# A graph network's compare operand moves to PSUM, and the node sums move to the banks of their transposes

## The reference

```python
edge_index = stack([src, dst])
x = x + L0(relu(norm(x)), ...)   # attention: score = q[dst]*k[src] per head, softmax over the
                                 # edges of a node, sum of weight * v[src], then @ Wa
x = x + L1(relu(norm(x)), ...)   # 4 layers: relu(x[src] + silu(edge_attr @ We + be)), segment_sum
                                 # over dst, two matmuls with silu, layer norm
x = x + L2(relu(norm(x)), ...)   # 2 convolutions with degree norm: segment_sum of rows, @ W, relu
x = x + L3(relu(norm(x)), ...)   # segment_sum(x[src]) @ W + x @ W_self
```

## Time and profile before

| | |
|---|---|
| median of 3 runs | 11198.52 us (11189.39 to 11209.08) |
| profiled execution | 11231.99 us, span 11230.1 us |
| busy in the span | PE 6020.5 us (54%), DVE 3251.3 (29%), ACT 1365.6 (12%), POOL 6472.3 (58%) |
| granted PE clock, mean over the span | 0.723 of full speed |
| DMA | 960.66 MB, mean 86 GB/s |
| comparisons of L1327 | 1567.8 us busy, 1969 of them, mean 796 ns |
| gathers of L700 into `rows` | 5386.0 us busy, 5488 of them, mean 981 ns |

### The profile page before, as it was taken

One profiled execution on the slowest core, in us unless ns is written; L12 is line 12 of the kernel. 1 busy time (PEld: TensorE's weight loads), 2 busy tenths in 40 slices (PEclk: granted clock), 3 DMA queues, 4 the chain that ended last, 5 costly groups with the idle time before them and its releaser, 6 DMA issues. The chain is left out here.

```text
span 11230.1 us, 158248 instructions
## 1 busy us (share of the span) xinstructions
PE 6020.5 (54%) x23911; PEld 4066.9 (36%) x23912; DVE 3251.3 (29%) x7438; ACT 1365.6 (12%) x2091; POOL 6472.3 (58%) x6737
## 2 busy tenths in 40 slices
PE   2556646566665666756666566653344333433344
PEld 1334425433443333433344333332333233333334
DVE  2334467612232122311223122331122112221222
ACT  1112210011221112211122111210000000000000
POOL 2556526466655665556554655546666566656665
PEclk9566669877887788877888778875666555665566
DMA  4777754233322333323332322221111111111111
GB/s 112 206 208 218 219 152 129 86 85 83 84 80 73 86 82 80 82 74 86 82 80 75 83 80 79 77 57 44 46 47 47 44 44 46 44 42 44 45 46 44
DMA packets 982683, 960.66 MB, mean 86 GB/s; under 512 B 442720, under 2 KB 710395, under 8 KB 982137
## 3 DMA queue, kind: packets, MB, share of 16 engines
q0 software_dynamic: 213248, 462.82, 15.6%
q1 hardware_dynamic: 647644, 399.74, 13.3%
q10 hardware_dynamic: 121756, 97.77, 2.7%
HBM read 801.39 MB, written 164.71 MB: 86 GB/s over the span
## 5 line engine op out<-in xcount | busy, mean ns | idle before, releaser
L700 POOL DMA_INDIRECT rows<-node_rows,idx x5488 | 5386.0, 981 | 3647.5 <-SPq L550 1992.6
L1327 DVE SCALAR_TENSOR_TENSOR onehots<-iota_f,win_base,dst_ch 128x512 f32<-128x512 f32 x1969 | 1567.8, 796 | 6664.0 <-remote 3954.8
L832 PE MATMUL ps_seg<-rows,onehots 128*128 x7840 | 1584.2, 368 | 2422.8 <-DVE sums L1348 1089.9
L832 PEld LDWEIGHTS ps_seg<-rows,onehots 128*128 128x128 f32 x7840 | 1383.6, 265 | 2621.6 <-issue 2617.4
L832 PEld LDWEIGHTS ps_seg<-onehots 128*128 128x128 f32 x7840 | 1178.7, 220 | 1744.6 <-issue 962.5
L832 PE MATMUL ps_seg<-onehots 128*128 128x128 f32 x7840 | 1231.4, 307 | 1066.6 <-DVE sums L1348 466.6
L906 PE MATMUL ps_big<-q_res,ident 128*128 (+1 forms) x1968 | 1277.0, 736 | 766.1 <-issue 325.5
L906 PE MATMUL ps_big<-rows,ident 128*128 (+1 forms) x1968 | 1180.7, 686 | 2.1 <-issue 2.1
L700 POOL DMA_INDIRECT sums<-kv_rows,idx x784 | 775.2, 989 | 528.5 <-SPq L550 302.6
L1051 ACT ACTIVATE onehots<-ps_big 128x512 f32<-128x512 f32 x980 | 576.1, 597 | 3251.0 <-remote 1470.5
L906 PEld LDWEIGHTS ps_big<-rows,ident 128*128 128x128 f32 x1968 | 445.1, 227 | 616.3 <-issue 614.0
(11 more groups left out here) (193 smaller groups left out, 2243.4 us busy)
## 6 DMA issues: line engine op xcount, KB each, us to landing
q_res<-gates_by_edge SPq DMA_DIRECT2D x784, 256.0 KB
rows<-node_rows,idx POOLq DMA_INDIRECT x5488
gates_by_edge<-gate ACTq DMA_DIRECT2D x244, 256.0 KB
rows<-dst_padded SPq DMA_DIRECT2D x196, 256.0 KB
value_rows_by_edge<-sums SPq DMA_DIRECT2D x196, 256.0 KB
rows<-value_rows_by_edge SPq DMA_DIRECT2D x196, 256.0 KB, 3.1
idx<-src_padded SPq DMA_DIRECT2D x1568, 2.0 KB
node_rows<-h_res ACTq DMA_DIRECT2D x49, 448.0 KB
```

The costliest lines, as they stand in the source:

```text
L700: pool.indirect_dma_start(target[:, r, j, :], None, table, bass.IndirectOffsetOnAxis(ap=idx[:, r, j:j + 1], axis=0)).then_inc(rows_landed[ ...
L832: last = nc.tensor.matmul(ps_seg[u % 2][:, 0:width], onehots[:, u, j, :], rhs(j), start=j == 0, stop=j == J - 1)
L1327: V.scalar_tensor_tensor(onehots[:, u, :, :], iota_f[:, :].rearrange("p (a n) -> p a n", a=1).to_broadcast([P, J, P]), win_base[:, ds(w, 1 ...
```

## The change

A name `numbers` is given to the first 128 columns of bank `ps_mm[0]`. DVE copies `iota_f` into them once, just ahead of the attention pass. `mark_edges` reads its node numbers from there instead of from SBUF; its other tensor input `dst_ch`, its per-partition operand `win_base` and its output stay in SBUF. The sums of L856 are written to `ps_sum`, another name for `ps_t`, and DVE's `summed(h)` reads them there; `ps_mm[1]` is no longer used from the attention pass on.

```diff
+        numbers = ps_mm[0][:, 0:P]
+        ps_sum = ps_t
...
-                            last = nc.tensor.matmul(ps_mm[h][:, (i - a) * D:(i - a + 1) * D], left, right,
+                            last = nc.tensor.matmul(ps_sum[h][:, (i - a) * D:(i - a + 1) * D], left, right,
                                                     start=m == 0, stop=m == len(pairs) - 1)
...
+            chain(V.tensor_copy(numbers, iota_f[:, :]))
+
             def mark_edges(k, s, u, c, w):
 
                 V.scalar_tensor_tensor(onehots[:, u, :, :],
-                                       iota_f[:, :].rearrange("p (a n) -> p a n", a=1).to_broadcast([P, J, P]),
+                                       numbers.rearrange("p (a n) -> p a n", a=1).to_broadcast([P, J, P]),
                                        win_base[:, ds(w, 1)],
                                        dst_of(c).rearrange("p (j a) -> p j a", a=1).to_broadcast([P, J, P]),
                                        ALU.add, ALU.is_equal).then_inc(onehot_ready, 1)
...
-                return ps_mm[h][:, 0:(end - first) * D].rearrange("p (w d) -> p w d", d=D)
+                return ps_sum[h][:, 0:(end - first) * D].rearrange("p (w d) -> p w d", d=D)
```

## The result

The changed kernel takes 11240.85 us in the median of 19 runs (11210.81 to 11270.77). The kernel before took 11225.04 us on the same chip (19 runs, 11188.83 to 11240.41). The ratio on record is 1.0022, with an interval of 1.0011 to 1.0032. It is not the quotient of the medians, which is 1.0014: the kernel is slower by 16 us by the medians and by some 25 by the ratio, at the edge of what can be told. Forecast were 11050 us and a range that ended at 11185.

What follows compares the result with a forecast made beforehand. The gather passes were taken as a chain of POOL gather runs, each followed by a nearly fixed release. Terms 0.3 - 105 - 45 + 0 = -150 us, from 11198.5, gave 11050 us; range 10950 to 11185.

Steps and rivals of the forecast that it cites:

- The price of a comparison: L1327 on DVE: reading one input from PSUM changes its time by 0, between -1 and +4 ns each.
- Its effect on POOL: Gather passes: 161 us of gather stretching removed, mean gather 981 to 952 ns; attention: POOL's copy nearer 202 ns.
- The moved sums: L856's sums written to ps_t: same instructions and width, no semaphore wait added for L844, 0 us.
- rival B: Comparison's operands left in SBUF still hold POOL, so nothing is freed: 11198 us; chance 0.10.
- rival D: PSUM as a source is dear for DVE's comparisons; 76 ns each would cancel the 150 us; chance 0.05.
- One check of the prediction: DVE operations of 512 columns: two SBUF inputs would take 688 ns, as with one input in PSUM.
- Attention: Attention pass: DVE and POOL no longer exclude each other; half of at most 87 us gained, -45 us.
- the 161 us: Seven gather passes: stretching of gathers put down to L1327; two thirds, 105 us, would shorten the kernel, bounds 0 and 161.
- of nearly fixed length: Gather passes: each run of gathers is followed by a release whose length hardly changes, some 3 us after the run.
- rival C: Gather passes: denser gathers lengthen the releases; 0.5 us more per slot wait gives 11293 us; chance 0.07.
- Rival A: Only the attention pass gains; gather runs shorten but POOL waits longer for slots: 11153 us; chance 0.12.

Runs made afterwards that it cites:

- e12_extra_sbuf: Changed kernel plus one 512-column DVE operation, both inputs in SBUF, behind each gather-pass comparison; on chip D 9259.06 us, ratio 1.0014.
- e13_extra_psum: As e12_extra_sbuf, but one input of the added DVE operation is in PSUM; on chip D 9067.57 us, ratio 0.9808.
- e2_attention_only: Changed kernel, moved sums kept, but the comparison reads its numbers from PSUM in the attention pass only; 11056.97 us, ratio 0.9978 to the kernel before.
- e3_three_gathers: Three of each chunk's four gathers issued from the attention pass on, so some summed rows are stale; 9253.92 us, ratio 0.8342 to the kernel before.
- e4_slower_pool: Changed kernel plus a POOL memset and a wait for it ahead of each chunk's gathers; 10968.65 us, ratio 0.9887 to the kernel before.
- e10_long_pause: As e6_attention_pause, but two memsets, each waited for, ahead of each chunk's gathers; 10938.59 us, ratio 0.9758 to the kernel before.
- e17: The kernel of e12_extra_sbuf run again on a slower chip; 11134.92 us, ratio 1.0041 to the kernel before.
- e18: The kernel of e13_extra_psum run again on the same slower chip as e17; 11183.24 us, ratio 1.0082 to the kernel before.
- e6_attention_pause: e2_attention_only plus a POOL memset and a wait for it ahead of each chunk's gathers; 10937.72 us, ratio 0.9858 to the kernel before.
- e5_before_pause: Kernel before plus a POOL memset and a wait for it ahead of each chunk's gathers; 10941.13 us, ratio 0.9872.

## Why the prediction was wrong

**Right.** The price of a comparison: 0 was forecast, and it takes 750 ns where it took 752. Its effect on POOL: the gathers' mean falls to 949 ns (952 forecast), 178 us of stretching are gone (161 forecast), the copy takes 215 ns (near 202). The collision itself shows in the traces: of the gathers before, 930 start inside a comparison and take 1124 ns on average, the others 952; in the changed kernel 927 do so and take 943. In attention the comparison falls to 750. The moved sums cost nothing; L848 takes 320 ns for 309, and no wait on DVE of note appears ahead of it (6.4 and 5.5 us, 5.4 and 4.1 before). So rival B (nothing is freed) falls, and rival D (PSUM is dear) in its form of a longer comparison. One check of the prediction was none: it derived 688 ns for 512 columns from SBUF with a slope that took the 688 ns of the PSUM form as its start. e12 and e13 supply the comparison, 684 and 680 ns.

**Mis-sized.** Attention was put at -45 us, between 0 and 87; it is -23 in the traces and -24 by the ratio of e2_attention_only. Only PE's wait for DVE's sums shrank, by 26 us. Its wait for POOL's products, which I counted in part, did not, although POOL's copies save 37 us and its products 9: half of that goes into longer waits for its loads (190.3 to 213.8 us), which rival B had named for this pass, and the other half is the 23 us.

**The step that failed** is the one on how much of the 161 us comes through: "I take two thirds, 105 us", drawn from "In such a chain a gather that gets shorter makes the pass shorter, though POOL idles". On the chip of the result none of it came through: -178 us of gathers, +167 us of slot waits, and 42 us on top. Taken as a fact about the work the sentence holds. e3_three_gathers shows that fewer gathers shorten a pass, and e13_extra_psum against e12_extra_sbuf that shorter ones do, one for one, where no end is held back. What it left out is that the release is not "of nearly fixed length". On the slower chips it depends on the gaps that POOL leaves between gathers. Pauses that cost 1071 us of POOL's time gave 1254 back (e4_slower_pool), and the long pause brought the unexplained waits down to 815 us (e10_long_pause). The explanation that fits is that a stretched gather, which waits for DVE, was a small pause at no cost. That last step is argued and not shown: the idle gaps that were shown to help are 0.8 us or longer, a stretched gather adds 0.18 on average, and a cost of the PSUM source that arises on these chips alone would give the same sign in e2 against the changed kernel and in e17 against e18.

That was rival C, which stood at 0.07 with the words "nothing in the rows shows that a pause helps". The rows did hold a sign of it: the release came only when the run of gathers was over the earlier trace rows. I read from it that the run delays the release and not that the release needs the run to stop. C's price was too high, though: it reckoned with 0.5 us per slot wait and 11293 us. Measured were 167 / 493 = 0.34 us, just past its 0.31, which takes up the gathers' gain, and the slot waits do not account for the remaining 42 us, of which some may be chance: the score pass, which the change does not touch, moved by 9 us between the two traces. Rival A, only attention gains, is right on where the gain is and wrong on the total, 11153 us.

**What stays open.** Shown is that the loss sits in the source of the comparison in the gather passes, that pauses between POOL's gathers shorten the single held release, and that one chip of five has none. Why sequencers of SyncE, PE and DVE take 0.7 us for an instruction in the passes with gathers, on those chips and not on D, no run shows. Nor does one show by what road the PSUM source raises their number: a kernel on a slower chip whose gathers are kept as long as before in another way, with the source in PSUM, would tell. The comparison of e17 with e18 is on one slower chip, and its two kernels have an additional DVE operation, so the 0.4% are borne out by two roads, e2 against the changed kernel, whose chips may differ, and e17 against e18. The changed kernel itself did not run on D; from the pair there it should gain some 2%, an estimate.

**The better version.** On the slower chips e2_attention_only (0.9978), e6_attention_pause (0.9858) and e10_long_pause (0.9758) beat both kernels. On D the pauses lose 11 to 13%. e2_attention_only is the careful choice: its attention pass is 497 us long on D too, in the windows of e13_extra_psum, where that pass is the same code, and the gather passes are left as they were.

```profile
1437.00:1934.00 497.00, 317.77 (x2107) 276.94 (x2107) 317.04 (x785) 14.65 (x22) 241.47 (x393) 0.90 0.39 113
3973.00:4994.00 1021.00, 771.31 (x3119) 473.19 (x3119) 459.13 (x1052) 256.38 (x349) 743.93 (x785) 0.90 0.39 105
```

The second row is an edge pass on D: 1021 us, where it took 1330 in the changed kernel, with the same 744 us of gathers.

## What to carry to other kernels

Before work is taken off an engine that waits, find out what its idle time does for others: add a pause to it in one experiment and work of the same length in another, and see which way the time goes. A wait that no record explains is not a fixed cost to be built into a sum; until its cause is known, both signs belong into the range. And run on more than one chip: the same operand moved to PSUM was worth -2.1% on one and +0.4% on another.

## What the runs showed of the hardware

- A source in PSUM costs DVE nothing over one in SBUF at 512 columns: 750 ns against 752, and 680 against 684 for the added two-input operation.
- A gather that starts during a DVE operation with two SBUF inputs waits for that operation's end: in the kernel before those that start 0.1 to 0.7 us into a comparison end 0.82 us after it in the median. One takes 1.38 us for 0.95 in the earlier trace rows, and in e5_before_pause, whose timeline has one in both rounds from 8604 to 8612; the second:

```profile
8610.39 0.75 DVE L1331 SCALAR_TENSOR_TENSOR onehots<-iota_f,win_base,dst_ch 128x512 f32<-128x512 f32 x1 [5.21 <-PE ps_seg L836]
8610.50 1.46 POOL L704 DMA_INDIRECT rows<-node_rows,idx  x1 [0.30 <-issue]
```

  With one input in PSUM it takes 0.94. The Trainium skill, "SBUF — State Buffer", Who interferes with whom, has a DVE instruction with at most one SBUF input leave GpSimd alone, and the trace agrees now with this second half too. The page also infers that a `tensor_tensor` does not hold up the writing of DMA descriptors. Here gathers are held up by one: e12_extra_sbuf's take 984 ns on average, e13_extra_psum's 949. A gather also reads its indices from SBUF, and no run tells which of the two is held.
- Five chips ran the kernel before in 11214, 11094, 11092, 11087 and 9249 us. The last one's gathers are no faster (949 ns in e13_extra_psum); what differs is that its traces hold none of the unexplained waits and next to none of the instructions of 0.7 us.
- On the slower chips those instructions of SyncE, PE and DVE come with POOL's gathers: 3982 of 67011 in the seven gather passes and none of 7868 in the attention pass of the kernel before.
